# A graph network kernel whose edge stage is written out instead of looped

## The reference

```python
msg_input = jnp.concatenate([node_i, node_j, edge_features], axis=-1)
h = jax.nn.relu(msg_input @ mW1 + mb1)                      # 512 wide, one row per edge
messages = h @ mW2 + mb2
aggregated = jax.ops.segment_sum(messages, i_idx, num_segments=node_features.shape[0])
```

## Time and profile before

| What | Value |
|---|---|
| Time, median of 3 runs | 2491.06 us (2490.74 to 2491.39) |
| The profiled execution | 2493.28 us, of which the span from the first to the last instruction is 2491.5 us |
| PE busy | 2097.7 us (84%) |
| DVE busy | 1692.2 us (68%) |
| POOL busy | 1180.9 us (47%) |
| ACT busy | 814.3 us (33%) |
| Mean granted clock of PE | 0.883 of full speed |
| The edge stage in the span | from about 583 to 1512 us |

### The profile page before, as it was taken

One profiled execution on the slowest core, in us unless ns is written; L12 is line 12 of the kernel. 1 busy time (PEld: TensorE's weight loads), 2 busy tenths in 40 slices (PEclk: granted clock), 3 DMA queues, 4 the chain that ended last, 5 costly groups with the idle time before them and its releaser, 6 DMA issues. The chain is left out here.

```text
span 2491.5 us, 38886 instructions
## 1 busy us (share of the span) xinstructions
PE 2097.7 (84%) x9567; PEld 1297.5 (52%) x9568; DVE 1692.2 (68%) x5369; ACT 814.3 (33%) x2430; POOL 1180.9 (47%) x1453
## 2 busy tenths in 40 slices
PE   4677666644888988898888988999996999999999
PEld 2333333321333433343333434776774888888887
DVE  7987767665777877777778777777775444454454
ACT  1222121112444544454444444554561500200100
POOL 3777777774444444444444445998992200000000
PEclk7667766766999999999999998999995999999999
DMA  3111111113444444444444444111122244243343
GB/s 111 44 50 44 44 44 52 44 38 95 127 129 133 138 127 125 132 136 130 127 127 138 129 128 126 59 61 56 60 66 80 75 138 119 85 138 109 95 145 101
DMA packets 185517, 243.01 MB, mean 98 GB/s; under 512 B 35932, under 2 KB 154265, under 8 KB 185386
## 3 DMA queue, kind: packets, MB, share of 16 engines
q0 software_dynamic: 45968, 119.96, 17.0%
q1 hardware_dynamic: 108258, 96.17, 13.3%
q10 hardware_dynamic: 31160, 25.32, 3.1%
HBM read 196.40 MB, written 44.86 MB: 97 GB/s over the span
## 5 line engine op out<-in xcount | busy, mean ns | idle before, releaser
L957 POOL DMA_INDIRECT brow<-B_rows,rows x416 | 397.5, 956 | 494.1 <-DVE pre L1053 483.8
L383 POOL DMA_INDIRECT src_list<-ring,ring_row x392 | 412.9, 1053 | 153.5 <-issue 117.0
L1731 PE MATMUL pO<-F,y 128*128 128x512 f32 (+1 forms) x2100 | 473.2, 381 | 12.1 <-DVE y L1622 11.6
L995 PE MATMUL pNode<-hid,oh 128*128 128x512 f32 x832 | 453.6, 628 | 0.6 <-ACT hid L1016 0.6
L1731 PEld LDWEIGHTS pO<-F,y 128*128 128x128 f32 x2100 | 371.9, 189 | 83.9 <-DVE y L1622 13.6
L1016 ACT ACTIVATE hid<-pre 128x512 f32<-128x512 f32 x416 | 262.0, 630 | 405.3 <-DVE pre L1053 405.3
L1039 DVE TENSOR_TENSOR S<-S,pNode 128x512 f32 x416 | 285.9, 687 | 115.6 <-PE pNode L995 72.0
L988 PE MATMUL pEdge<-A,turned 128*128 x1248 | 360.1, 398 | 0.0
L1053 DVE TENSOR_TENSOR pre<-pEdge,brow 128x512 f32<-128x512 f32 x416 | 282.6, 679 | 101.8 <-PE pEdge L988 101.7
L1592 DVE CAST F<-raw 128x512 fp32r<-128x512 uint16 (+1 forms) x525 | 206.0, 396 | 186.6 <-PE pO L1731 181.7
L1171 POOL TENSOR_SCALAR src_oh<-iota,src_s 128x128 bf16<-128x128 bf16 x473 | 304.4, 658 | 29.4 <-PE pC L1340 28.0
(11 more groups left out here) (281 smaller groups left out, 3008.0 us busy)
## 6 DMA issues: line engine op xcount, KB each, us to landing
raw<-C_rows SPq DMA_DIRECT2D x90, 640.0 KB, 4.0
C_rows<-c_rows ACTq DMA_DIRECT2D x175, 114.5 KB, 1.7
rows<-src_list SPq DMA_DIRECT2D x104, 100.0 KB, 2.1
brow<-B_rows,rows POOLq DMA_INDIRECT x416, 3.4
B_rows<-bst SPq DMA_DIRECT2D x25, 256.0 KB, 2.1
src_list<-ring,ring_row POOLq DMA_INDIRECT x392, 2.2
hT_rows<-hT SPq DMA_DIRECT2D x25, 128.0 KB, 1.8
resid<-in_x_dram SPq DMA_DIRECT2D x1, 3072.0 KB
```

The lines of the kernel that those rows point to most:

```text
L383: nc.gpsimd.indirect_dma_start(dr.src_list[:, :, :].rearrange("p t w -> (p t) w"), bass.IndirectOffsetOnAxis(ap=ring_row[:, k % RING, t:t ...
L957: nc.gpsimd.indirect_dma_start(brow[:, t % BR, :], None, dr.B, bass.IndirectOffsetOnAxis(ap=rows_i[:, b, j, 1:2], axis=0)).then_inc(b_in[t ...
L995: mm(pN[j % 2][:, :], oh32[:, (j - 2) % 4, :], hid[:, j % 2, :], start=True, stop=True).then_inc(node_done, 1)
L1731: last = mm(pO[n % 2][half][:, 0:width(c)], y_part(win, part, half), F[:, (n * NW + win) % FS, 0:width(c)], start=(win == 0 and part == 0) ...
```

## The change

PE, ACT and DVE no longer loop: all 416 tiles are written out, so every tile number, buffer index and semaphore value is a constant. `blocks` is gone. `windows` now loads eight block numbers, always beginning at a multiple of eight. PE loads those of tiles 0 to 7 at the start and then, for every t that is a multiple of 8, those of tiles t to t+7 at the end of step t, behind the matmuls of that step; their first use is in step t+1. DVE loads them at the start of step t and uses them from step t+4 on. Tiles, buffers, matmuls, waits between engines and the SP and POOL programs stay as they were.

```diff
-def windows(nc, eng, tile_map, i, lag, unroll):
+def windows(nc, eng, tile_map, first, n):
+
     _, got = nc.values_load_multi_w_load_instructions(
-        tile_map[0:1, bass.ds(first, n)], engines=[eng.engine], min_val=0, max_val=NW - 1,
+        tile_map[0:1, first:first + n], engines=[eng.engine], min_val=0, max_val=NW - 1,
         skip_runtime_bounds_check_because="the map counts at most NW - 1 windows before a tile")
-    return {skip + k: w for k, w in enumerate(got)}
+    return {first + k: w for k, w in enumerate(got)}
...
-            def step(i, j):
-                t = T * i + j
-                if j == 0:
-                    win.clear()
-                    win.update(windows(nc, pe, keep.src_map, i, 1, T))
+            win = windows(nc, pe, keep.src_map, 0, GRP)
+
+            for t in range(NT + 2):
+                j = t % T
...
-                if inside(i, j - 2, T, NT):
+                if inside(t - 2, NT):
                     pe.wait_ge(hid_ready, t - 1)
...
-                    mm(pN[j % 2][:, :], oh32[:, (j - 2) % 4, :], hid[:, j % 2, :], start=True, stop=True
+                    mm(pN[t % 2][:, :], oh32[:, (t - 2) % 4, :], hid[:, t % 2, :], start=True, stop=True
                        ).then_inc(node_done, 1)
-
-            blocks(pe, NT + 2, T, 1, LAST, step)
+                if t % GRP == 0 and 0 < t < NT:
+                    win.update(windows(nc, pe, keep.src_map, t, GRP))
...
-            blocks(act, NT + 1, T, 1, LAST, step)
...
-                if j == 0:
-                    win.clear()
-                    win.update(windows(nc, dve, keep.src_map, i, 4, T))
-                if inside(i, j - 4, T, NT):
+                if t % GRP == 0 and t < NT:
+                    win.update(windows(nc, dve, keep.src_map, t, GRP))
+                if inside(t - 4, NT):
...
-            blocks(dve, NT + 4, T, 1, LAST, step)
```

More of the change, by code:

```diff
@@ L60, with inside @@
 assert LEAD + 2 * NW + 1 < BLOCKS and BINS <= 256
[L63 to L79, removed]
-def windows(nc, eng, tile_map, i, lag, unroll):
[L84 to L90, removed]
+def inside(t, n):
+    return 0 <= t < n
+def windows(nc, eng, tile_map, first, n):
     _, got = nc.values_load_multi_w_load_instructions(
-        tile_map[0:1, bass.ds(first, n)], engines=[eng.engine], min_val=0, max_val=NW - 1,
+        tile_map[0:1, first:first + n], engines=[eng.engine], min_val=0, max_val=NW - 1,
         skip_runtime_bounds_check_because="the map counts at most NW - 1 windows before a tile")
-    return {skip + k: w for k, w in enumerate(got)}
+    return {first + k: w for k, w in enumerate(got)}
 class Names:
@@ L934, in edge_mlp @@
         s_added = g.sem("s_added")
-        LAST = NT // T - 1
+        GRP = 8
         block = stack.enter_context(nc.Block())
@@ L964, in _ @@
             mm = nc.tensor.matmul
-            win = {}
-            def step(i, j):
-                t = T * i + j
-                if j == 0:
-                    win.clear()
-                    win.update(windows(nc, pe, keep.src_map, i, 1, T))
-                if inside(i, j, T, NT):
+            win = windows(nc, pe, keep.src_map, 0, GRP)
+            for t in range(NT + 2):
+                j = t % T
+                if inside(t, NT):
                     pe.wait_ge(oh_ready, 2 * t + 2)
-                    if not isinstance(i, int) or t >= 2:
+                    if t >= 2:
                         pe.wait_ge(turn_copied, t - 1)
@@ L979, in step @@
                                         keep.ident16[:, :]).then_inc(turn_done, 1)
-                if inside(i, j - 1, T, NT):
-                    b = (j - 1) % 2
+                if inside(t - 1, NT):
+                    b = (t - 1) % 2
                     pe.wait_ge(turn_copied, t)
-                    if not isinstance(i, int) or t >= 3:
+                    if t >= 3:
                         pe.wait_ge(pre_ready, t - 2)
-                    w = win[j]
+                    w = win[t - 1]
                     mm(pE[b][:, :], turned[0:EW, b, P:2 * P], keep.we[:, :], start=True, stop=False)
@@ L990, in step @@
                     last.then_inc(edge_done, 1)
-                if inside(i, j - 2, T, NT):
+                if inside(t - 2, NT):
                     pe.wait_ge(hid_ready, t - 1)
-                    if not isinstance(i, int) or t >= 4:
+                    if t >= 4:
                         pe.wait_ge(s_added, t - 3)
-                    mm(pN[j % 2][:, :], oh32[:, (j - 2) % 4, :], hid[:, j % 2, :], start=True, stop=True
+                    mm(pN[t % 2][:, :], oh32[:, (t - 2) % 4, :], hid[:, t % 2, :], start=True, stop=True
                        ).then_inc(node_done, 1)
-            blocks(pe, NT + 2, T, 1, LAST, step)
+                if t % GRP == 0 and 0 < t < NT:
+                    win.update(windows(nc, pe, keep.src_map, t, GRP))
         @block.scalar
         def _(act):
-            def step(i, j):
-                t = T * i + j
-                if inside(i, j, T, NT):
+            for t in range(NT + 1):
+                j = t % T
+                if inside(t, NT):
                     act.wait_ge(turn_done, t + 1)
-                    if not isinstance(i, int) or t >= 2:
+                    if t >= 2:
                         act.wait_ge(edge_done, t - 1)
                     nc.scalar.activation(turned[:, j % 2, 0:P], pT[j % 2][:, 0:P], ACT.Copy,
-                                         accum_out=keep.tile_deg[:, bass.ds(t, 1)])
+                                         accum_out=keep.tile_deg[:, t:t + 1])
                     nc.scalar.copy(turned[0:EW, j % 2, P:2 * P], pT[j % 2][0:EW, P:2 * P]).then_inc(turn_copied, 1)
-                if inside(i, j - 1, T, NT):
-                    b = (j - 1) % 2
+                if inside(t - 1, NT):
+                    b = (t - 1) % 2
                     act.wait_ge(pre_ready, t)
-                    if not isinstance(i, int) or t >= 3:
+                    if t >= 3:
                         act.wait_ge(node_done, t - 2)
                     nc.scalar.activation(hid[:, b, :], pre[:, b, :], ACT.Relu).then_inc(hid_ready, 1)
-            blocks(act, NT + 1, T, 1, LAST, step)
         @block.vector
@@ L1026, in _ @@
             win = {}
-            def step(i, j):
-                t = T * i + j
-                if j == 0:
-                    win.clear()
-                    win.update(windows(nc, dve, keep.src_map, i, 4, T))
-                if inside(i, j - 4, T, NT):
+            for t in range(NT + 4):
+                j = t % T
+                if t % GRP == 0 and t < NT:
+                    win.update(windows(nc, dve, keep.src_map, t, GRP))
+                if inside(t - 4, NT):
                     dve.wait_ge(node_done, t - 3)
-                    if not isinstance(i, int) or t > 4:
+                    if t > 4:
                         dve.wait_ge(s_added, t - 4)
-                    sw = S[:, bass.ds(win[j] * HID, HID)]
+                    sw = S[:, bass.ds(win[t - 4] * HID, HID)]
                     v.tensor_tensor(sw, sw, pN[j % 2][:, :], ALU.add).then_inc(s_added, 1)
-                if inside(i, j, T, NT):
-                    if j % LC == 0:
-                        dve.wait_ge(rows_in[j // LC], 16 * (i + 1))
+                if inside(t, NT):
+                    if t % LC == 0:
+                        dve.wait_ge(rows_in[j // LC], 16 * (t // T + 1))
                     lo = rows[:, j // LC, j % LC, 0:1]
@@ L1046, in step @@
                     v.tensor_scalar(oh32[:, j % 4, :], keep.iota[:, :], lo, None, ALU.is_equal).then_inc(oh_ready, 1)
-                if inside(i, j - 2, T, NT):
-                    b = (j - 2) % 2
+                if inside(t - 2, NT):
+                    b = (t - 2) % 2
                     dve.wait_ge(edge_done, t - 1)
-                    dve.wait_ge(b_in[(j - 2) % BR], 16 * (i * (T // BR) + (j - 2) // BR + 1))
-                    if not isinstance(i, int) or t >= 4:
+                    dve.wait_ge(b_in[(t - 2) % BR], 16 * ((t - 2) // BR + 1))
+                    if t >= 4:
                         dve.wait_ge(hid_ready, t - 3)
```

## The result

The changed kernel takes 2350.11 us, the median of 4 runs (2347.8 to 2354.04), against 2490.9 us of the kernel before in the same comparison. The ratio is 0.9441, with a 95% interval of 0.9422 to 0.946: 5.6% faster. The forecast was 2350.5 us. The profiled execution of the changed kernel took 2354.04 us, its span is 2352.2 us, and its mean granted clock 0.903.

A forecast was written before the change was run, and what follows sets the result against it. PE was taken as the bound inside turns, with the loss at their ends: 140.4 us there plus 0.5 us at the stage's start, 140.9 us off 2491.06, gave 2350.2, forecast 2350.5 us (range 2344 to 2375).

The forecast's parts named there:

- The bound and the size of the loss: Edge stage: PE bounds a turn's inside; turn ends lose 5.62 us a boundary, 140.4 us in all.
- slack built up in the gaps: Sign of failure: a steady tile of 1.9 us or more would mean warm turns lived on this, above all DVE's.
- PE's load: PE's register load of block numbers in the edge stage: eight would take 0.59 us, against 3804 ns for sixteen.
- The cover: At a group's end, line 995's matmuls would hide PE's load, with 0.15 us to spare.
- The clock: PE in the edge stage: without idle time it would not fall to the lower level, gaining about 2.0 us a boundary.
- The 2.0 us a boundary: Slow-clock share of the 5.62 us lost at each turn boundary, left after the stall of 3.61 us.
- DVE's load: DVE's loads of eight in the edge stage: 0.59 us each and hidden; upper bound 0.3 us times 51, 15 us.
- The stage's start: DVE's first load, ahead of the first one-hot matrix, would fall from 1105 ns to 0.59 us: 0.5 us gained.
- Code fetching: Written-out code in the edge stage: some 36 more fetches on PE's queue, costed at nothing.
- rival 3: Fetching the code stalls PE in the edge stage: 49 us if each fetch showed in full, 2399 us; chance 0.05.
- What is late next: In the edge stage POOL's gathers would still wait for DVE's `pre`, having slack at 1.85 us a tile.

The follow-up runs named there:

- e5_from_one_above: The changed kernel, but PE's loads of eight begin one element above a multiple of eight, in a map copy moved up by one: 2409.82 us, ratio 0.9671.
- e2_loop_aligned: The kernel before with its loop, but PE's loads of sixteen begin at a multiple of sixteen, from a map copy moved up by one: 2377.54 us, ratio 0.9554.
- e7_sixteen_aligned: The changed kernel, but PE loads sixteen numbers from a multiple of sixteen at every sixteenth step, not eight at every eighth: 2359.99 us, ratio 0.9472.
- e3_written_old_loads: The changed kernel, written out, but with the old loads of sixteen on PE and DVE from the kernel before: 2463.77 us, ratio 0.99.
- e6_old_dve_loads: The changed kernel, but DVE loads sixteen numbers at every sixteenth step as before, PE's loads staying new: 2360.89 us, ratio 0.9475.

## Why the prediction was right, point by point

*The bound and the size of the loss.* The bound was the right one, though the slices were read too evenly: from 10 to 24 the busy digit is 8 or 9 and not 8 throughout; nothing in the sum rests on it. 1.851 us a tile came from one warm turn of 26 us; the stage now runs at 1.852 for 763 us. 140.4 us were forecast for the tiles. In the profile the way from the fourth to the last tile is 903.0 - 763.2 = 139.8 us shorter. No slack built up in the gaps had carried the warm turns.

*PE's load.* 0.59 us was the step on which all hung, and it is 591 ns. The row of another stage with the same engine, count and kind of start was the right one to take; half of 3804 ns would have put the forecast near 2411 us, and e5_from_one_above shows that such a kernel runs at 2410. e2_loop_aligned shows the load as the cause inside the old loop, so this is shown and not argued. The Trainium skill (Runtime: NRT & Kernel Launch, section Instruction fetch mechanics) has about 200 ns a register even in bulk, said beside the register loads of the preamble. For the loads of this kernel, from on-chip memory, the measurement agrees for loads from a bad start (234 ns) and not for the others (64 ns a register in fours).

*The cover.* I had 0.15 us to spare, and it is 0.28 at the load shown and about 0.2 by the longer loads. In e7_sixteen_aligned the load is 0.51 us longer and 0.28 of it shows; in e5_from_one_above it is 1.34 us longer and 1.13 shows (57.4 us over 51 loads).

*The clock.* It stays up, as forecast. The 2.0 us a boundary were a remainder, not a row, but the timeline of the kernel before bears them out. Behind the gap of the earlier trace rows that ends at 982.37 the next two tiles start at

```profile
985.95 0.31 PE L977 MATMUL pTurn<-ident,oh 128*128 128x128 bf16 x1
...
988.99 0.22 PE L977 MATMUL pTurn<-ident,oh 128*128 128x128 bf16 x1
```

so they took 3.58 and 3.04 us instead of 1.84. Over the 25 boundaries the loss behind the gap is 1.6 to 3.0 us, 2.09 on average; in e3_written_old_loads, with its shorter gap, it is 1.54.

*DVE's load.* 596 ns and hidden, as forecast. But "nothing or little of it reaches PE" at 1.11 us was wrong: 0.28 us do (e6_old_dve_loads). I had looked at the path over the one-hot matrix, whose weight load had 0.43 us in hand; the delay came over `pre` and the hidden rows. It was a bound only, and the range had it.

*The stage's start.* Here I was off. I expected the first tile at 595.8 and it came at 596.6: the first load of DVE in this stage takes 853 ns and not 596, and the stage began half a microsecond later. The fourth tile was early all the same (601.91 against 602.59), because the clock rose sooner (the two float32 matmuls ahead of it take 1.13 us in the timeline instead of 1.91). Behind the edge stage the kernel takes 987.1 us from the last transposes to the end, against 985.9 before. These small terms, -0.7 and +1.2 us, are within the spread of the runs.

*Code fetching.* Forecast: 36 more fetches on PE's queue and no idle time. The page of the kernel after, and its fetches from 600 to 1360 us:

```profile
q8 instruction: 90, 1.47, 0.3%
...
q8 instruction: 35, 0.57, 0.3%
```

There are 31 more than the 59 of before, and PE is busy for 739.93 of 740 us from 620 to 1360 us, with these fetches beside it, so rival 3 is out.

*What is late next.* The gathers still wait for DVE, as in the earlier trace rows, from 620 to 1360 us at 156 GB/s:

```profile
POOL brow L936 <- DVE pre L1025: 328.6, 388, 1.1
```

*The hit itself.* That 2350.5 us came within 0.4 us of the median is luck: the four runs lie between 2347.8 and 2354.04 us. Between the two profiles the span is 139.3 us shorter (2491.5 - 2352.2), against 140.9 in the sum. What was right is the terms, each to within about a microsecond.

## What to carry to other kernels

Look at what the sequencer does in an idle time that ends with "issue" before the loop is blamed: here one register load begun at a bad element made 116 of the stage's 140 us, and moving its data by one element got them back with the loop in place. Begin register loads at a multiple of four numbers, read no more at once than the matmuls already handed out will cover (0.8 us here), and put the load right behind them. For the price of an instruction take the row with the same engine, count and alignment, also from another stage, and not a share of a larger one; for the pace after the change take the stretch in which the bounding engine has no idle time.

## What the runs showed of the hardware

- A register load on PE takes 0.08 us and 0.257 us for every four numbers where it begins at a multiple of four; numbers left over at the end, and all numbers where it begins elsewhere, take about 0.234 us each. Sixteen numbers are 1.10 or 3.81 us by this alone. DVE's sixteen from such a multiple take 1.10 us as well. The first load of the edge stage took 0.19 us (PE) to 0.26 us (DVE) longer than the later ones; in the next stage the first load on PE took 593 ns, no longer than the rest.
- PE's clock stayed at its upper level through 51 idle times of 0.97 us, fell behind 5 of 50 of 1.9 us and behind all 25 of 2.8 us.
- Some 9100 instructions of PE written out (6656 matmuls and weight loads, the rest waits and address arithmetic), with 35 fetches in 760 us, cost PE nothing, at 156 GB/s of other transfers.
